# A mixture-of-experts, attention, mixture-of-experts kernel: lot counts, first weights and last steps put in other places

## The reference, cut to what matters

```python
x = x + 0.5 * ffn(layernorm(x), ...)     # x: 16 sequences x 256 tokens x 128
x = x + attn(layernorm(x), ...)          # 16 heads of 8, rms norm and rope on q and k, full softmax
x = x + 0.5 * ffn(layernorm(x), ...)

def ffn(x, Wr, br, W1, b1, W2, b2):      # 8 experts, 128 -> 512 -> 128
    expert_idx = argmax(xf @ Wr.T + br)  # each of the 4096 tokens goes to one expert
    h = relu(einsum('td,efd->etf', xf, W1) + b1)
    y = einsum('etf,edf->etd', h, W2) + b2
    return y[expert_idx, arange(4096)]
```

## Time and profile before

| | us |
|---|---|
| median of three runs | 461.86 |
| the profiled execution | 463.23 |
| its span, first to last instruction | 461.4 |
| busy: TensorE / VectorE / ScalarE / GpSimd | 419.0 / 374.3 / 350.3 / 327.3 |

### The profile page before, as it was taken

One profiled execution on the slowest core, in us unless ns is written; L12 is line 12 of the kernel. 1 busy time (PEld: TensorE's weight loads), 2 busy tenths in 40 slices (PEclk: granted clock), 3 DMA queues, 4 the chain that ended last, 5 costly groups with the idle time before them and its releaser, 6 DMA issues.

```text
span 461.4 us, 13980 instructions
## 1 busy us (share of the span) xinstructions
PE 419.0 (91%) x4123; PEld 313.4 (68%) x4123; DVE 374.3 (81%) x992; ACT 350.3 (76%) x815; POOL 327.3 (71%) x528
## 2 busy tenths in 40 slices
PE   7889999989888899999999999999888989999996
PEld 4347999878665555655656556656555549998996
DVE  4895787998797788888898888998887786876774
ACT  4416777787756798999999889998777877776773
POOL 8019898888857879868687477557967634677756
PEclk9999999999999899999999999999999999999999
DMA  7882334252100000000000000000001122133310
GB/s 208 264 298 58 84 97 148 70 175 63 31 26 11 14 26 9 14 9 14 14 9 9 3 1 4 5 3 1 20 28 44 37 67 62 54 104 100 97 40 22
DMA packets 28649, 27.02 MB, mean 59 GB/s; under 512 B 5684, under 2 KB 25947, under 8 KB 28018
## 3 DMA queue, kind: packets, MB, share of 16 engines
q1 hardware_dynamic: 24034, 17.65, 12.9%
q0 software_dynamic: 4544, 8.49, 6.8%
HBM read 16.56 MB, written 12.71 MB: 63 GB/s over the span
## 4 chain that ended last, share of the span: by engine, by line
PE 48%; DVE 22%; issue 13%; ACT 8%; DMA 3%; POOL 2%; DVEq 1%; SPq 1%; POOLq 1%; ACTq 0%
PE PS L932 10%; PE PS L916 10%; DVE Smax L1897 9%; PE PS L1063 7%; PE PS L1016 5%; PE PS L1039 5%; ACT Pt L1306 3%; PE PS L998 3%; PE PS L982 3%; DVE St L1463 2%; PE PS L905 2%; PE PS L1093 1%; ACT QkT L1200 1%; DVE HsT L1740 1%; DMA XX<-x 1%
## 5 line engine op out<-in xcount | busy, mean ns | idle before, releaser
L1897 DVE TENSOR_REDUCE Smax<-PS 128x4 f32<-128x1024 f32 x128 | 156.1, 1224 | 32.2 <-PE PS L1016 31.2
L1306 ACT ACTIVATE Pt<-PS 128x1024 f32<-128x1024 f32 x128 | 126.2, 1024 | 18.5 <-PE PS L1039 15.3
L932 PE MATMUL PS<-W,HsT 128*128 x624 | 84.1, 278 | 2.0 <-DVE Ys L1751 2.0
L916 PE MATMUL PS<-XsT,Ws 128*128 128x128 f32 x624 | 83.2, 276 | 0.7 <-ACT XsT L1200 0.5
L916 PEld LDWEIGHTS PS<-XsT,Ws 128*128 128x128 f32 x624 | 76.4, 192 | 4.3 <-ACT XsT L1200 1.4
L932 PEld LDWEIGHTS PS<-W,HsT 128*128 128x128 f32 x624 | 76.1, 192 | 4.3 <-issue 3.4
L1063 PE MATMUL PS<-Pt,Vg 128*32 128x256 f32 x1024 | 68.5, 385 | 0.5 <-DVE Lg L1919 0.3
L730 POOL TENSOR_TENSOR HL<-Rn,Zero 128x512 fp32r<-128x512 f32 x28 | 35.4, 1284 | 37.5 <-DVE Rn L1880 35.9
L1016 PE MATMUL PS<-QkT 24*128 24x256 f32 x512 | 59.6, 305 | 1.9 <-DVE Smax L1897 1.7
L638 POOL DMA_INDIRECT Pt<-rows,TokI x39 | 40.5, 1038 | 28.4 <-DVE TokI L1692 19.8
L1016 PEld LDWEIGHTS PS<-QkT 24*128 24x128 f32 x512 | 40.0, 184 | 27.6 <-ACT Pt L1306 22.8
(11 more groups left out here) (277 smaller groups left out, 727.7 us busy)
## 6 DMA issues: line engine op xcount, KB each, us to landing
AtCol<-slots SPq DMA_DIRECT2D x39, 65.5 KB, 1.8
rows<-XX SPq DMA_DIRECT2D x8, 288.0 KB, 4.3
XX<-x SPq DMA_DIRECT2D x8, 256.0 KB, 4.5
W<-w1T SPq DMA_DIRECT2D x2, 1024.0 KB, 6.1
W<-w2T SPq DMA_DIRECT2D x2, 1024.0 KB, 9.1
mid<-mid_second SPq DMA_DIRECT2D x1, 1472.0 KB
mid<-Ys SPq DMA_DIRECT2D x16, 64.0 KB
QkT<-NmaxT SPq DMA_DIRECT2D x64, 4.0 KB
```

What stands on the lines that cost most here:

```text
L916: last = nc.tensor.matmul(PS[:, h_bank(n) + c // 2, (c % 2) * P:(c % 2 + 1) * P], Ws[:, n % R_WS, c * P:(c + 1) * P], XsT[:, n % 2, :], st ...
L932: last = nc.tensor.matmul(PS[:, y_bank(n), 0:P], HsT[:, n % 2, c, :], W2[:, ds(e * D_FF + c * P, P)], start=(c == 0), stop=(c == FC - 1))
L1306: nc.scalar.activation(Pt[:, m % 2, 2 * pair:2 * pair + 2, :, :].rearrange("p h c t -> p (h c t)"), PS[:, score_bank(m, pair):score_bank(m ...
L1897: nc.vector.tensor_reduce(Smax[:, b % 2, :, at:at + 33:32].rearrange("p t h -> p h t"), PS[:, max_bank(m, pair):max_bank(m, pair) + 2, :]. ...
```

## The change

The steps of the lots and of their stores:

```diff
-LARGEST_AT = {38: 0, 48: 1, 59: 2}
-TIES_AT = {39: 0, 49: 1, 59: 2}
-PICK_AT = {42: 0, 50: 1, 59: 2}
-SEEN_AT = {43: 0, 51: 1, 59: 2}
-RANK_AT = {45: 0, 52: 1, 62: 2}
-POOL_SLOT_AT = {45: 0, 54: 1, 62: 2}
+LARGEST_AT = {38: 0, 50: 1, 59: 2}
+TIES_AT = {39: 0, 51: 1, 59: 2}
+PICK_AT = {42: 0, 51: 1, 59: 2}
+SEEN_AT = {44: 0, 52: 1, 59: 2}
+RANK_AT = {48: 0, 54: 1, 62: 2}
+POOL_SLOT_AT = {48: 0, 54: 1, 62: 2}
-STORE_AT = {45: (0,), 47: (1, 2), 48: (3, 4), 50: (5, 6), 51: (7, 8), 52: (9, 10), 53: (11,),
+STORE_AT = {48: (0, 1), 49: (2,), 50: (3, 4), 51: (5, 6, 7), 52: (8, 9), 53: (10, 11),
             54: (12, 13), 55: (14, 15), 56: (16, 17), 57: (18, 19),
             62: (20, 21), 63: (22, 23, 24), 64: (25,)}
-FILL_MAXIMA = {58: 6}
+LAST_PROJECT = 3
+LAST_MAXIMA, SCORES_AHEAD = 58, 61
-LAST = {"norm": 0, "inverse": 5, "rank": 9}
+LAST = {"norm": 0, "inverse": 4, "rank": 8}
-        POOL_LOTS = 6
+        POOL_LOTS = 5
```

GpSimd copies the first weights, in its step 59 (VectorE's `weights`, with the same copies, is taken out):

```diff
+            def first_weights():
+                pool.wait_ge(slots_ready, 2)
+                for t in range(R_WS):
+                    n = S_TILES + t
+                    e = pool.value_load(tile_expert(1, t), min_val=0, max_val=N_EXP - 1)
+                    nc.gpsimd.tensor_copy(Ws[:, n % R_WS, :], W1[:, ds(e * D_FF, D_FF)]).then_inc(ws_ready, 1)
+                    nc.gpsimd.tensor_copy(Bs[:, bias(n), :], B1T[:, ds(e * FC, FC)]).then_inc(bs_ready, 1)
```

TensorE's last steps: `values(57)` comes ahead of the last maxima's transpose, the fill is gone, and the first pair of scores of groups 61, 62 and 63 is computed a step earlier (`first_scores(m + 1)` at the end of `scores(m)`):

```diff
                 if in_pairs(m):
-                    products((0, 1)).then_inc(score_ps, 1)
-                    pe.wait_ge(exp_ready, 2 * m)
-                    products((2, 3)).then_inc(score_ps, 1)
+                    if m < SCORES_AHEAD:
+                        first_scores(m)
+                    second_scores(m)
+                    if SCORES_AHEAD <= m + 1 < N_ALL:
+                        first_scores(m + 1)
...
-                if n in FILL_MAXIMA:
-                    fill_const(FILL_MAXIMA[n], bank_of("nmaxT", seq(n, 2)))
...
+                if n == LAST_MAXIMA:
+                    values(n - 1)
                 if n < 0 or not group(n + QKT_LEAD):
                     small(n)
                 if n == TAIL - 1:
                     first()
-                if group(n - 1):
+                if group(n - 1) and n != LAST_MAXIMA:
                     values(n - 1)
```

In the first expert layer ScalarE copies the third tile's weights behind the first relu instead of ahead of it:

```diff
                     w_copy(0)
                     x_evacuate(0)
-                    for t in range(1, R_WS):
-                        w_copy(t)
+                    w_copy(1)
...
+                        if not k and t == 0:
+                            w_copy(2)
```

In the last stage, VectorE takes the residual and statistics of the last sequence in tile 3 ahead of the tile's `scale`, not behind its output; ScalarE's last inverse deviation stands in tile 4 behind the weight copy, not in tile 5 behind the relu; the last rank is in tile 8, and VectorE takes it at `(8, 2)` instead of `(9, 0)`, and starts on the table at `(9, 0)` instead of `(9, 2)`:

```diff
+                        if k and t == LAST_PROJECT:
+                            step(*DRAIN[t])
...
-                            if t > 1:
+                            if 1 < t < LAST_PROJECT:
                                 for n in DRAIN.get(t, ()):
                                     step(n)
...
-                if (t, place) == (9, 0):
+                if (t, place) == (8, 2):
                     dve.wait_ge(*filled("rank", i))
...
-                if (t, place) == (9, 2):
+                if (t, place) == (9, 0):
```

More of the change, by code:

```diff
@@ L1025, in max_transpose, with score_products, rows_ready @@
                 last.then_inc(filled("nmaxT", b)[0], 1)
-            def scores(m):
-                b, g = divmod(m, N_GRP)
+            def score_products(m, heads):
+                for c in range(SEQ_TILES):
+                    for h in heads:
+                        rows = slice(32 * h, 32 * h + SPLIT + 1)
+                        last = nc.tensor.matmul(PS[:, score_bank(m, h // 2) + h % 2, c * T:(c + 1) * T],
+                                                QkT[rows, m % R_QK, 1, c * P:(c + 1) * P],
+                                                QkT[rows, m % R_QK, 0, :], start=True, stop=True)
+                return last
+            def rows_ready(m):
                 pe.wait_ge(max_in[m % R_QK], 16 * (m // R_QK + 1))
@@ L1066, in values @@
                     last.then_inc(filled6, 1)
+                elif m == SCORES_AHEAD - 1:
+                    last.then_inc(values_ps, 1)
             def y_transpose(b):
@@ L1396, in step @@
                     second_copy(n - 1)
-                if not late(n) and n not in FILL_MAXIMA:
+                if not late(n) and n != LAST_MAXIMA:
                     small_copy(n)
@@ L1804, in run @@
                                 low(0)
-                return weights, begin, run
+                return begin, run
             def reload(i):
@@ L1962, in step @@
                     lot_take(RANK_AT[n])
-                if n == WEIGHTS_AT:
-                    weights()
                 if n in LARGEST_AT:
@@ L2072, in _ @@
             route()
-            weights, begin, run = experts(0)
+            begin, run = experts(0)
             begin()
             run()
-            weights, begin, run = experts(1)
+            begin, run = experts(1)
             for n in range(RAMP_END, TAIL):
```

36 lines of the change are left out of this document (19 added, 17 removed).

## The result

The changed kernel took **471.20 us** (median of 4, 470.39 to 471.90) against 462.13 for the kernel before beside it (461.74 to 462.61): ratio **1.018** (95% interval 1.016 to 1.020). I had said 460.8, with a range to 463.0 and a chance of 0.14 for slower. Later batches of the same kernel gave 463.71 to 473.62, so its single executions spread over 10 us while most of the kernel before's lie within 4. What varies with them is the granted clock: the mean over an execution of the clock that TensorE was given, as a share of 2.4 GHz. Ratios and their intervals are worked out from the executions within some 1.5% of the fastest of their kernel and so leave out some of the low ones, while the medians hold all and the counts of low executions all but four far-off ones (583 to 1332 us). Each batch had the kernel before beside it.

The account below looks back on a forecast made before the run. No single engine bounds the attention but a loop through TensorE, VectorE and ScalarE. Gains of 0.1 + 0 + 0.2 + 0 + 0.8 = 1.1 us off 461.86 gave 460.8 us, range 458.7 to 463.0.

Parts of the forecast that it names:

- First layer: ScalarE's third copy goes behind the relu, so the second tile's evacuation starts sooner: 0.1 us gained, between 0 and 0.2.
- Lot 5: Step 2, its terms moved from VectorE to GpSimd: 0 for the median, bounds 0.4 us lost and 1.2 gained.
- rival 2: Last steps: TensorE idle without the fill, so the clock falls, worth 1.2 us: 462.0 us, chance 0.2.
- Lots 0 and 1: Steps 43 to 52, side work moved to other steps: net 0.2 us gained, from 0.5 lost to 1.0 gained.
- its place in steps 50 to 52 costs at most 0.1, as the old operations stood there: Cost of lot 1's `HotE` in its new place, set against 0.5 us gained by leaving step 48.
- third rival: GpSimd's copies of weights hold VectorE's last lot, which ends 1.6 to 3 us later: 463.2 us, chance 0.13.
- The stores: Two more GpSimd stores behind step 50's split make lot 2's variance and logits 2.56 us later.
- Steps 58 to 62: Scores ahead (0.5 us) just pay for the later lot: 0; 1.7 to 1.9 gained if logits were not late.
- GpSimd's copies: Copies of weights in the last steps: 0.6 us for one input of 512, bounds 0.4 and 1.28.
- A rule against it: Shared ports: every GpSimd weight copy holds VectorE's lot for its whole length; the sum had only the first, for 0.3 us.
- Last stage: Last residual a tile earlier removes the late tile's 1.03 us stall, less 0.25: 0.8 us gained, bounds 0 and 1.0.
- a fall is worth 1.2 us as above: Price of a clock fall in the last steps, taken from the one fall seen at step 2.

Follow-up runs that it names:

- b_tables: The kernel before with the new tables of the lots' steps and of the stores alone: 463.52 us, ratio 1.001.
- a_again: The changed kernel itself run again in more executions: 469.62 us, ratio 1.014.
- b_last: The kernel before with the last steps' part alone (first weights by GpSimd, `values(57)` first, no fill, scores ahead): 460.06 us, ratio 0.995.
- a_lot6: The changed kernel with lot 5's layernorm terms back on VectorE (POOL_LOTS 6): 462.64 us, ratio 1.000.
- b_end: The kernel before with the last stage's part alone (last residual at tile 3, inverse deviation at 4, rank at 8): 462.55 us, ratio 1.000.
- b_lt: The kernel before with the fifth lot on GpSimd and the new tables, nothing else: 465.30 us, ratio 1.007.
- best1: The changed kernel with the old tables and lot 6 as GpSimd's first: 459.44 us, ratio 0.993.
- a_oldtab: The changed kernel with the old tables, the fifth lot still on GpSimd: 461.13 us, ratio 0.998.
- a_pad24: The changed kernel with 24 one-column memsets in GpSimd's idle time ahead of step 43's copies: 463.21 us, ratio 1.000.
- a_pad8: The changed kernel with 8 one-column memsets in GpSimd's idle time ahead of step 43's copies: 463.17 us, ratio 1.000.
- best2: The changed kernel with the old tables and lot 5's inverse deviation a step later: 459.28 us, ratio 0.992.

## Why the prediction was wrong

**First layer**, 0.1 gained: not shown. In the profiles the start of step 0 lies anywhere from 142.0 to 144.1 in kernels with and without this part (147.6 in the two with the stretch at 134), which is far more than the term.

**Lot 5**, 0: mechanism right, price wrong. GpSimd's variance was to come a little late. It did, and step 2 took 4.92 us where kernels without the fall and without lot 5 took 4.60: 0.3 lost, within my bounds (0.4). Part of it is the operation of 0.68 us that ran beside VectorE's `Rn`. What I did not price is the idle time of TensorE that this brings, 1.14 us in place of 0.66. I had even noted, under rival 2, that such idle time goes ahead of a fall, and applied it to the last steps alone. Of the nine profiles with this wait of 1.1 us, four have a fall in step 3 or 4 (3.4, 3.4, 6.8 and 17.1 us); of the ten without it, none.

**Lots 0 and 1**, 0.2 gained: 0.74 in `b_tables` (0.42 + 0.49 + 0.13 - 0.14 - 0.16). The scan and `Run` were unheld in step 44, which I had as a bound. But the sentence "its place in steps 50 to 52 costs at most 0.1, as the old operations stood there" is **a step that failed**. It holds only while GpSimd's copies stay where they were. In the changed kernel they came beside the pick, which took 1.60 us and not 0.26, and steps 52 to 54 took 1.1 us more even where no fall came (`a_again`). It is the mechanism of my third rival (GpSimd holds VectorE), some 30 us ahead of where I looked for it. In all seven profiles with a slow pick (0.91 to 1.60 us) it ended 0.09 us behind the end of GpSimd's second copy (347.66 against 347.57 above), whenever it had begun; in four of them it began while the first copy still ran, and it was held through both. The rule of the Trainium skill ("SBUF — State Buffer", section "SBUF: two separate sides") that I had weighed against a row of 0.81 us fits this: the pick reads two operands in SBUF.

**The stores**: 2.56 us predicted, 2.5 measured. **Steps 58 to 62**, 0: -1.9 without the tables (`b_last`), +0.45 with them alone, +2.0 with both in `a_lot6`, with TensorE at 1.2 GHz for 6.8 us. So the 0 was off by 2 us, and that `a_lot6` is at 1.000 is luck: 0.8 us gained in steps 44 to 49 and 1.0 behind step 63 happen to pay for it. The later stores and lot were as worked out, but the clock fell there as in rival 2, to which I gave 0.2, and in nine of the ten profiles of kernels with both the tables and the new last steps. GpSimd's copies: 0.6 predicted, 0.61 measured. VectorE's small operations were held by 0.8 us together, not 0.3 (L1604 0.48 us and L1611 0.57 where they took 0.24 before, and `Run` 0.41, not 0.17): each of the three copies held one of them to its own end, as the paragraph "A rule against it" had it.

**Last stage**, 0.8 gained: not shown. The stretch is 0.65 shorter in `b_end`'s profile and 1.1 in the changed kernel's, but as short in `b_lt`, which lacks the part, and the time of `b_end` is that of the kernel before (0.999 to 1.002).

**The clock** is the term that made most of the 9 us, and its price is **the other step that failed**: "a fall is worth 1.2 us as above". I took it from one short fall, and took a fall for something that is there or not. For that length it is right: step 2 took 5.87 us with a fall of 3.4 us in it (5.88 in `best1`) and 4.60 without. But a fall has a length: 3.4, 6.8, 17.1, 20.5 and 27.3 us were seen. In steps 3 to 6 they cost 1.5 us for 3.4 (`a_oldtab`, `b_lt`), 2.7 for 6.8 (`a_pad24`) and 6.6 for 17.1, which is most of the 8.0 us between the two spans. Without long stretches the sum would still have missed: `a_pad8` and `a_pad24` are at 463.2, 2.4 above my 460.8 and just outside the range, of which 0.6 to 2.3 lie in steps 58 to 62. The wait for instructions itself I could not have read from the profile of before, but a bound for GpSimd being late ahead of the `HL` copies I could have given: 2 us of lateness brings two copies of 1.28 us beside VectorE's pick.

What is shown: in the changed kernel the fifth lot and the tables must come together for most executions to be low (10 of 12, against 0 of 10 and 1 of 10 with one of them undone); where the instructions stand in GpSimd's stream decides the 2.4 us; the lateness of GpSimd's copies decides the length of the pick. What is argued from counts alone: that the idle times of TensorE start the long stretches. Against it stand `a_lot6`, `b_lt` and `best2` in the table. What stays open: why a fall lasts 3.4 us in one execution and 27 in the next with the same instructions, and where the stretches of unprofiled executions lay. Only two low executions of the changed kernel were profiled, and they had them at the two seats.

## What to carry to other kernels

An engine with slack has a timetable: before you move a side job on it, list what of it runs beside what on the other engines, and ask what each pair costs if one comes 2 us late. Where two constants are harmless alone and cost 2% together, compare the kernels step by step first; the step that differs in the pair, and in an undisturbed execution too, is the place. And before you give a fall of the clock a price, look at several executions: price it by its length and by how many executions have it, not by one profile.

## What the runs showed that I had not expected

- Eight tiny instructions more on GpSimd, in idle time, made this kernel 6 us faster (463.17 against 469.62 in an earlier batch); its first store was then 0.97 us behind the slots and not 3.3.
- One two-operand operation of VectorE on 64 elements took from 0.26 to 1.60 us, by what GpSimd did beside it, and was held through two operations of GpSimd that followed each other, not only through the one that was running.
- TensorE stayed at 1.2 GHz for up to 27.3 us while it was busy 26.36 of them.
